# A metaformer block on one core: another order in the third slot, weights set up behind the first turning, and a fourth buffer for x

## What is computed

```python
def block(x):                                   # x (4, 64, 128, 128), 8 heads
    n = ln_over_channels(x, eps=1e-6)
    k, q, v = relu(Wk @ n + bk), relu(Wq @ n + bq), Wv @ n + bv
    context = einsum('bhkn,bhvn->bhkv', k, v)   # over all 16384 tokens of an image
    x = x + Wr @ einsum('bhkv,bhkn->bhvn', context, q) + br
    t = tokens(x)
    u = ln_over_tokens_channels(t, eps=1e-5)
    p = softmax(u @ router_w + router_b)        # 8 experts
    top_p, top_i = top_k(p, 2); top_p /= sum(top_p)
    return x + from_tokens(sum over the two of top_p * (u @ expert_w + expert_b))
```

## Time and profile before

| | before |
|---|---|
| median of 3 runs | 672.26 us (671.27 to 673.7) |
| the profiled execution | 671.9 us |
| its span, first to last instruction | 670.1 us |
| TensorE busy | 616.2 us (92%) |
| VectorE busy | 515.1 us (77%) |
| ScalarE busy | 425.2 us (63%) |
| GpSimd busy | 396.1 us (59%) |
| mean granted TensorE clock | 0.992 |
| longest chain, by engine | PE 62%, DVE 18%, ACT 10% |

### The profile page before, as it was taken

The page is one execution under the profiler, slowest core; times in us unless marked ns, Lnnn a source line. Parts: engine busy times, 40 slices in busy tenths (PEclk is TensorE's granted clock), DMA queues, the critical chain, the costliest instruction groups (busy, mean ns, idle before and its releaser), DMA issues.

```text
span 670.1 us, 21498 instructions
## 1 busy us (share of the span) xinstructions
PE 616.2 (92%) x8318; PEld 276.3 (41%) x8318; DVE 515.1 (77%) x1176; ACT 425.2 (63%) x832; POOL 396.1 (59%) x350
## 2 busy tenths in 40 slices
PE   3799989779999999999999999999999999998887
PEld 1566656444444444444444444444332332332222
DVE  3534455978888888889788787987799999989844
ACT  2355545576666675766757576766766776766642
POOL 7232342237565655666666556655577777777875
PEclk9799989999999999999999999999999999999999
DMA  6223635666555566655545665554565667446542
GB/s 149 56 76 79 146 97 129 150 167 159 122 122 134 126 147 146 159 142 138 133 111 130 147 152 127 129 116 104 133 154 127 157 172 170 101 111 142 126 111 48
DMA packets 32662, 86.21 MB, mean 129 GB/s; under 512 B 7650, under 2 KB 7826, under 8 KB 32562
## 3 DMA queue, kind: packets, MB, share of 16 engines
q1 hardware_dynamic: 32082, 84.64, 52.8%
q0 software_dynamic: 288, 0.19, 0.2%
q10 hardware_dynamic: 192, 0.01, 0.0%
HBM read 34.47 MB, written 16.78 MB: 76 GB/s over the span
## 4 chain that ended last, share of the span: by engine, by line
PE 62%; DVE 18%; ACT 10%; issue 7%; DMA 1%; POOL 1%; ACTq 0%; DVEq 0%; SPq 0%; POOLq 0%
PE bank L1092 26%; PE bank L1078 7%; PE bank L1015 5%; PE bank L993 4%; PE bank L979 4%; DVE z L826 3%; PE bank L938 3%; PE bank L1089 3%; PE bank L962 3%; DVE x L731 3%; ACT grows L569 2%; DVE xnT L686 2%; PE bank L1039 2%; DVE osb L836 2%; ACT L529 2%
## 5 line engine op out<-in xcount | busy, mean ns | idle before, releaser
L442 POOL TENSOR_TENSOR z<-gbs,x1d 128x512 f32<-128x512 f32 x256 | 320.2, 1275 | 185.2 <-ACT gbs L575 72.6
L1095 PE MATMUL bank<-z,ew 128*64 128x512 f32 x512 | 243.7, 598 | 0.0
L1092 PE MATMUL bank<-z,ew 128*64 128x512 f32 x512 | 243.6, 598 | 0.0
L826 DVE TENSOR_TENSOR z<-bank,x1d 128x512 f32<-128x512 f32 x256 | 164.7, 675 | 16.2 <-PE bank L1078 16.2
L575 ACT COPY gbs<-bank 128x512 f32<-128x512 f32 x256 | 140.7, 594 | 43.8 <-PE bank L1078 41.3
L433 POOL TENSOR_TENSOR xsq<-xin 128x512 f32<-128x512 f32 x64 | 65.4, 1043 | 81.7 <-DMA xin<-in_x_dram 76.0
L1078 PE MATMUL bank<-grows,sel 64*64 64x512 f16 x1024 | 93.2, 387 | 16.3 <-ACT grows L569 7.3
L1092 PEld LDWEIGHTS bank<-z,ew 128*64 128x64 f32 x512 | 64.9, 136 | 104.6 <-issue 96.3
L503 ACT COPY xn<-bank 128x512 f32<-128x512 f32 x64 | 34.4, 589 | 62.8 <-PE bank L938 62.8
L1095 PEld LDWEIGHTS bank<-z,ew 128*64 128x64 f32 x512 | 64.7, 136 | 0.0
L686 DVE TENSOR_TENSOR xnT<-bank,rstd 128x512 f32<-128x512 f32 x64 | 41.0, 682 | 30.2 <-PE bank L924 28.5
(11 more groups left out here) (135 smaller groups left out, 804.8 us busy)
## 6 DMA issues: line engine op xcount, KB each, us to landing
x1d<-x SPq DMA_DIRECT2D x128, 256.0 KB, 4.5
xin<-in_x_dram SPq DMA_DIRECT2D x64, 256.0 KB, 4.2
x_again<-in_x_dram SPq DMA_DIRECT2D x64, 256.0 KB, 4.2
out_dram<-osb SPq DMA_DIRECT2D x128, 128.0 KB, 2.4
k<-in_const_dram SPq DMA_DIRECT2D x1, 453.5 KB, 3.8
ew_nat<-in_L_ffn_expert_w_dram POOLq DMA_DIRECT2D x2, 64.0 KB, 6.4
sel<-in_const_sel_dram SPq DMA_DIRECT2D x1, 128.0 KB, 3.4
bk_rows<-bk_wide ACTq DMA_DIRECT2D x6, 1.0 KB, 1.7
```

The lines of the kernel that those rows point to most:

```text
L442: pool.tensor_tensor(z[:, 1, i % R_Z, :], gbs[:, i % R_Z, :], x1d[:, g % 2, 1, u * NT:(u + 1) * NT], ALU.mult).then_inc(z_pool, 1)
L826: dve.tensor_tensor(z[:, 0, i % R_Z, :], bank[:, :], x1d[:, g % 2, 0, u * NT:(u + 1) * NT], ALU.mult).then_inc(taken_of(("spread", i, 0)), 1)
L1092: pe.matmul(out_bank[0:C, :], ew[:, j, :], z[:, 0, i % R_Z, :], start=False, stop=(j == PAIRS - 1), skip_group_check=True).then_inc(prod_d ...
L1095: pe.matmul(out_bank[C:P, :], ew[:, j, :], z[:, 1, i % R_Z, :], start=False, stop=(j == PAIRS - 1), skip_group_check=True).then_inc(prod_d ...
```

## The change

Four things are changed. In slot 2 all engines take the first spreading before the queries, so the order is spreading, queries, attention, spreading. In slot 3 VectorE runs the gates ahead of the last three operations of `x_deviations`. At the start, TensorE and VectorE run `set_weights` inside step 2 behind the turning back of group 0, with the centring of the key and query weights in step 1; the set-up's banks are others, and GpSimd issues the key bias's transfers. x has four places instead of three, so x of group 3 is loaded ahead of the weights. Besides, ScalarE squares x1 in one instruction of 1024 columns.

```diff
-R_X, R_Q, R_X1, R_Z = 3, 9, 7, 4
+R_X, R_Q, R_X1, R_Z = 4, 9, 7, 4
@@ bank_uses, and in the same way make_queries/broadcast on TensorE, take_queries/copy_gates on ScalarE
             if k == 2:
+                for i in iterations(n, k + 1)[:1]:
+                    yield from (("spread", i, s) for s in range(S))
                 if real(n - L_KEYS):
                     yield from (("queries", n - L_KEYS, s) for s in range(S))
-                for i in iterations(n, k + 1)[:1]:
-                    yield from (("spread", i, s) for s in range(S))
...
-        setup_bank = [bank[0], *misc[3:6]]
+        setup_bank = [bank[0], bank[7], misc[2], misc[3]]
@@ GpSimd, behind the slots of a step (and taken out of ScalarE's spread_key_bias)
+                if n == 2:
+                    pool.wait_ge(set_dve, N_SET_CLEAR)
+                    pool.wait_ge(bias_spread, 3)
+                    for s in range(S):
+                        for k in range(3):
+                            pool.dma_start(bk_rows[C * s + k:C * s + k + 1, :, :], bk_wide[0:1, k, :, :]
+                                           ).then_inc(bias_in, 16)
@@ ScalarE
-            def square_x1(g, u):
-                when_taken(act, ("attended", g, u))
+            def square_x1(g):
+                for u in range(U):
+                    when_taken(act, ("attended", g, u))
...
+                nc.scalar.activation(x1sq[:, :], x1[:, g % R_X1, :], ACT.Square).then_inc(x1_squared, 1)
@@ VectorE
             for n in range(STEPS):
-                if n == L_TURN:
-                    set_weights()
                 for k in range(SLOTS):
+                    if n == L_COLS and k == 2:
+                        centre_weights()
+                    if n == L_TURN and k == 1:
+                        set_weights()
...
-                    if k == 3 and real(n - L_COLS):
-                        x_deviations(n - L_COLS, 4, N_XSTAT)
                     for phase, (k0, k1) in gates_by_phase.items():
                         if quad_in(n, k, phase) is not None:
                             gates(quad_in(n, k, phase), k0, k1)
+                    if k == 3 and real(n - L_COLS):
+                        x_deviations(n - L_COLS, 4, N_XSTAT)
@@ TensorE
             def set_weights():
                 b0, b1, b2, b3 = setup_bank
+                when_taken(pe, ("cols", 1, 0))
...
-                if n == L_TURN:
-                    set_weights()
                 for k in range(SLOTS):
...
                             turn_back(n - L_TURN)
+                        if n == L_TURN:
+                            set_weights()
```

More of the change, by code:

```diff
@@ L529, in root_x @@
                 nc.scalar.activation(xstat[:, 4, :], xstat[:, 3, :], ACT.Sqrt).then_inc(xstat_root, 1)
-            def square_x1(g, u):
-                when_taken(act, ("attended", g, u))
+            def square_x1(g):
+                for u in range(U):
+                    when_taken(act, ("attended", g, u))
                 if g:
                     when_filled(act, ("rows", g - 1 + L_ROUTE, 0))
-                nc.scalar.activation(x1sq[:, u * NT:(u + 1) * NT], x1[:, g % R_X1, u * NT:(u + 1) * NT], ACT.Square
-                                     ).then_inc(x1_squared, 1)
+                nc.scalar.activation(x1sq[:, :], x1[:, g % R_X1, :], ACT.Square).then_inc(x1_squared, 1)
             def root_dev(p):
@@ L586, in spread_key_bias @@
                                    ).then_inc(bias_spread, 1)
[L587 to L591, removed]
                 act.wait_ge(weights_in, 16 * N_LOADS)
@@ L619, in _ @@
                     if k == 2:
+                        for i in iterations(n, k + 1)[:1]:
+                            copy_gates(i)
                         if real(n - L_KEYS):
@@ L622, in _ @@
                                 take_queries(n - L_KEYS, s)
-                        for i in iterations(n, k + 1)[:1]:
-                            copy_gates(i)
                     for i in iterations(n, k + 1)[1 if k == 2 else 0:]:
@@ L632, in _ @@
                         if real(n - L_ATTEND):
-                            for u in range(U):
-                                square_x1(n - L_ATTEND, u)
+                            square_x1(n - L_ATTEND)
                     for phase, step in gate_steps.items():
@@ L847, in less_mean, with centre_weights @@
                     then(dve.tensor_scalar(w_cen[0:C, k, :], w_nat[0:C, k, :], w_mean[0:C, k:k + 1], None, ALU.add))
-            def set_weights():
-                b0, b1, b2, b3 = setup_bank
+            def centre_weights():
                 dve.wait_ge(identity_in, 16)
@@ L856, in set_weights @@
                 assert n_set[0] == N_SET_KQ
+            def set_weights():
+                b0, b1, b2, b3 = setup_bank
                 dve.wait_ge(weights_in, 16 * N_LOADS)
@@ L1008, in make_rows @@
                 if real(g):
-                    pe.wait_ge(x1_squared, (g + 1) * U)
+                    pe.wait_ge(x1_squared, g + 1)
                     parts += [(x1[:, g % R_X1, :], route_w[:, :]), (x1sq[:, :], route_square_w)]
@@ L1143, in _ @@
                             turn_back(n - L_TURN)
+                        if n == L_TURN:
+                            set_weights()
                     if k == 2:
+                        for i in iterations(n, k + 1)[:1]:
+                            broadcast(i)
                         if real(n - L_KEYS):
                             make_queries(n - L_KEYS)
-                        for i in iterations(n, k + 1)[:1]:
-                            broadcast(i)
                         if real(n - L_ATTEND):
```

## The result

| | before | after |
|---|---|---|
| median | 672.70 us (671.27 to 676.08) | 678.21 us (676.85 to 679.07) |
| span of the profiled execution | 670.1 us | 676.2 us |

The ratio is 1.0077, with a 95% interval of 1.0060 to 1.0093: the changed kernel is slower by 5.5 us, and in the two profiled executions by 6.1. In the changed kernel most lines moved by a few: TensorE's spreading L1078 is L1085, the bias matmul L1089 is L1096, attention L1039 is L1046, VectorE's product L826 is L828, the tail L652 to L654 is L654 to L656, the normalising L686 is L688, the first keys L955 are L962.

The account below looks back on a forecast made before the run. TensorE was taken as the bound; odd steps +10.8, even steps -4.0, steps 33 and 34 -1.0 and start +2.0 gave +7.8 on 671.9, forecast 680 us. Its own range was 676 to 683, 8 in 10 668.5 to 685.5.

Parts of the forecast that it names:

- Slot 2: Attention to bias matmul shortens with the spreading first: 0.48 us won in odd steps, 0.67 in even steps.
- The collision: Slot 3, odd steps: two tail operations of x_deviations, from 6.99 us, are held by GpSimd's products starting at 6.84.
- (b): Rival: one GpSimd product holds VectorE's tail, not two; odd steps cost 0.2 us each, total 670.5 us; chance 0.10.
- The price of an odd step: Slot 3: VectorE's product starts 1.35 us later, passed whole to TensorE; eight odd steps 17 to 31, +10.8 us.
- Even steps: Six even steps without folding win 0.67 us each, -4.0 us together; none taken for 18 and 26.
- The last steps: Steps 33 and 34, with queries but no x_deviations, win 0.48 us each: -1.0 us together.
- The start: Before the first keys: later weights and a chained set-up put keys at 28.7 us; +2.0 taken, between -1.5 and +3.4.
- (a): Rival: tail falls before GpSimd's product or the product starts later, so no collision; 661.5 us, faster; chance 0.12.
- (c): Rival: the tail's last operation is caught in even steps too, so they win nothing; 684.5 us; chance 0.08.
- (d): Rival: TensorE's wait does not set the step and nothing collides, only the start's cost is left; 674 us; chance 0.08.

Follow-up runs that it names:

- e5: Kernel before with only slot 2's new order (spreading, queries, attention, spreading) on all three engines: 668.54 us, ratio 0.9922.
- e1: Changed kernel with the tail of x_deviations put back ahead of the gates: 668.55 us, ratio 0.9927.
- e4: Changed kernel with ScalarE squaring x1 ahead of the gates' copies in slot 3, so GpSimd's product starts later: 662.19 us, ratio 0.9831.
- e3: Changed kernel with the tail of x_deviations behind the gates' first three operations: 661.16 us, ratio 0.9814.
- e2: Kernel before with only the tail of x_deviations moved behind the gates, slot 2 in its old order: 677.13 us, ratio 1.0050.
- e6: Kernel before with the new start, four places for x and the single square, slot 2 and tail as before: 674.35 us, ratio 1.0018.
- e7: Changed kernel with three places for x instead of four: 678.59 us, ratio 1.0074.
- e10: Kernel before, unchanged, run once more for a second profile: 671.75 us.
- e8: Kernel before with slot 2's new order and the tail behind the gates' first three operations, old start: 661.29 us, ratio 0.9817.

## Why the prediction was right

The forecast was 680.0 us, slower; 678.21 was measured. By its steps:

- **Slot 2.** Attention to bias matmul 1.17 and 2.00, as worked out from the earlier trace rows; the wait for the queries is gone. In odd steps that gain only moved GpSimd forward, as e5 and e1 show: with the tail in its old place the odd step stays at 18.73.
- **The collision.** GpSimd's product was forecast at 6.84 and stands at 6.85; the tail at 6.78, 6.99 and then held, it stands at 6.75, 6.89 and 8.20, with two operations held. e4 and e3 take the collision away from either side and both give 17.93. The margin was forecast as 0.15 us and is 0.04: L655 starts that little behind GpSimd, in every odd step of both profiles. A tail 0.04 us earlier could have met one product instead of two, rival (b), and the error of the forecast, 0.10 us at L655, was larger than that. That a collision comes was worked out; that it is two operations and not one was in part luck. By the rule of the Trainium skill (SBUF — State Buffer, section "SBUF: two separate sides"), that the one which starts first blocks the other for its whole length, both outcomes follow, and the rows of e2, e3 and e4 agree: 1.19 us when it starts behind GpSimd, 0.17 when ahead. At the start the rows can't tell: L846 stands at 17.24, GpSimd's `xsq` at 17.25, and L846 takes 1.19. Nor does a row show the rule's other half, GpSimd held by VectorE: in e2 its pair starts inside L653 and takes its usual 2.51 us.
- **The price of an odd step**: forecast +1.35, measured +1.19 (one step +0.96). VectorE's product came at 9.31, not 9.5: it starts as the held operation ends (320.13 against 320.21), where I had added up ends. Sum over eight: +9.3 for +10.8.
- **Even steps**: -0.67 was right where I took it. I took nothing for steps 18 and 26, and they won 0.66 each. Nothing is caught there: in e5, with the tail ahead, step 18 is as long (19.61) as in the changed kernel. Sum over eight: -5.4 for -4.0.
- **The last steps**: steps 33 to 42 gave -0.4 for -1.0: step 33 won 0.5, step 34 only 0.13, and step 37 lost 0.24. The last comes from none of the named parts of the forecast: step 37 is 0.24 longer in every kernel with the new start and its single square (e6 too) and in none without; which of the edits does it is not shown.
- **The start**: +2.0 was taken, and step 17 came 2.6 us later, 2.9 in the second pair of profiles. The chain at the start held as far as the normalising: the weights came at 15.8 (forecast 16.0) and L688 at 19.89 (19.8), for the centring took 0.7 us more than the 1.9 forecast and the tail 0.6 less. The first keys were late by 3.07 (forecast 2.4), and what was missing is the set-up, 5.25 us for 4.6, with matmuls of 0.42 us where before they took 0.27. The upper bound, +3.4, had allowed for a half clock there; whether it was one is not shown, for this profile's record of the clock begins only at 31.6 us. Of the 3.07 us 2.75 were back by step 11 in the first pair, where step 16 then took 2.7 us more; in the second pair the loss was 2.0 at step 11 and 1.5 in step 16. The prediction never looked at step 16: there, too, the tail's last operation meets GpSimd's first product, and then TensorE runs at half clock.

```profile
142.39 2.49 POOL L442 TENSOR_TENSOR z<-gbs,x1d 128x512 f32<-128x512 f32 x2 [13.16 <-ACT gbs L583]
142.56 1.13 DVE L656 SCALAR_TENSOR_TENSOR rstd<-xstat 128x16 f32<-128x16 f32 x1
143.62 1.27 DVE L828 TENSOR_TENSOR z<-bank,x1d 128x512 f32<-128x512 f32 x2
144.35 0.69 PE L1032 MATMUL bank<-k,rows_sb 128*128 128x128 f32 x2 [1.80 <-DVE z L828]
```

The granted clock from 144 to 148 us is 0.57 in both profiles of the changed kernel, after a wait of TensorE of 1.8 us; in the first profile of before it is 1.00 there. The row of the changed kernel:

```profile
144.00:148.00 4.00, 3.65 (x80) 2.55 (x82) 3.06 (x7) 1.01 (x4) 0.89 (x1) 0.57 0.85 196
```

How the 2.6 us divide over the edits stays open. Step 17 starts 1.4 us later than in the first profile of before with the start alone (e6), 1.8 with the tail alone (e2), 0.8 with the order alone (e5), 3.2 with three places (e7); e3 starts it 0.6 us earlier and e4 3.8 later, although neither has the collision in the odd steps. The two profiles of one kernel differ by 1.5 us at step 11. That the hold in step 16 is the tail's is shown; that the clock fell for it is not, since a lower clock near there is the rule: over 133 to 148 us the granted clock is 0.89 or 0.77 in every profile, e10 of the kernel before among them, and 1.00 only in the first profile of before. What may differ is what the lower clock falls on.

So the difference was forecast as +7.8 and was +6.05 in the profiles. The odd steps were put 1.5 too high and the even ones 1.4 too high, the start 0.6 too low and the last steps 0.6 too low; some of the errors cancel. The rivals: (a), no collision, is what e3 and e4 built, and there the runs gave 661.2 and 662.2 us for the 661.5 worked out. (b) is nearest to e2, though with another order. (c) and (d) did not occur.

In the stage where all parts run, little is left to win beside TensorE: from 190 to 450 us it is busy 257.2 of 260 us in e3, where it was 252.6 before. The best kernel is e3 or e8, 1.9% faster than before; e8 needs nothing of the new start.

```profile
190.00:450.00 260.00, 257.19 (x3626) 116.73 (x3618) 217.89 (x503) 183.21 (x345) 168.78 (x141) 1.00 0.57 139
```

## What to carry to other kernels

A short VectorE operation that reads two SBUF tiles has a price of 0.18 or of 1.2 us, and which one depends on where GpSimd's long operations stand. Before such operations are moved, or an engine that feeds GpSimd is made faster, lay both engines' order of time side by side and look for the gap; here, with the new order in slot 2, the tail belongs in the middle of the gates, and from step 17 to 33 it costs 6.5 to 6.7 us more ahead of them and 16 more behind them. And edits of a tight pipeline are to be tried together as well as alone: two that won 5.4 and 2.6 us won 12.1 as a pair, and another place for the same three operations made the first one's gain into a loss.

## What the runs showed of the hardware

Back to back operations of GpSimd leave no gap for a queue of VectorE operations. In the changed kernel the first held operation comes free as GpSimd's first product ends and finishes with it, but the next one already meets the second product (1.28 and 1.19 us, 0.03 us between them). So here each product of a pair holds one short VectorE operation, and the loss went with how many of them met a product, not with the 0.17 us of work in each. In e1 the first product ends while L654 runs (0.21 us), L655 takes 1.21 to the second one's end, and L656 0.17 behind it; in e2 the held operation was the last of its kind.

The half clock ahead of step 17 was unexpected too. It differed between two executions of the kernel before (1.00 and 0.94 over 140 to 150 us), while it fell in the same place in both of the changed one (0.83 and 0.83).
